# Routing weights for the experts by transposes, DRAM and broadcast loads in place of spreading matmuls

## What is computed

```python
scores = jax.nn.sigmoid(xt.astype(jnp.float32) @ gate_w.T)      # 16 experts
biased = scores + gate_b
_, idx = lax.top_k(biased, TOPK)                                # TOPK = 4
w = jnp.take_along_axis(scores, idx, axis=-1)
w = w / jnp.sum(w, axis=-1, keepdims=True) * ROUTE_SCALE        # 2.5
comb = jnp.zeros((T, N_EXPERTS)).at[jnp.arange(T)[:, None], idx].add(w)
# for every expert e, over all T tokens:
h = _silu_and_mul(xt @ w13_e.T)                                 # 64 inner columns
y = y + c_e[:, None] * (h @ w2_e.T)
# and one shared expert without a weight:
y = y + _silu_and_mul(xt @ w13_s.T) @ w2_s.T
```

## Time and profile before

| | |
|---|---|
| time before, median of 3 runs | 1105.42 us (1102.48 to 1107.36) |
| the profiled execution | 1107.76 us |
| its span, first to last instruction | 1105.8 us |
| mean granted clock of PE | 0.934 |
| busy: PE, PEld, DVE, ACT, POOL | 1010.0, 471.6, 570.1, 558.1, 154.5 us |
| DMA | 27.36 MB in 8542 packets |

### The profile page before, as it was taken

How to read it: one execution, slowest core, us unless ns; L and a number is a source line. 1 busy time by engine, 2 the same in 40 slices (tenths; PEclk the granted TensorE clock), 3 DMA queues, 4 the chain that set the end, 5 groups by cost and what they waited for, 6 DMA issues and landing times.

```text
span 1105.8 us, 21935 instructions
## 1 busy us (share of the span) xinstructions
PE 1010.0 (91%) x9584; PEld 471.6 (43%) x9592; DVE 570.1 (52%) x942; ACT 558.1 (50%) x767; POOL 154.5 (14%) x168
## 2 busy tenths in 40 slices
PE   6679998989999999987989799998999999999998
PEld 3446665343333334775433243433433333353443
DVE  3665663463333447556546454455666665425454
ACT  4213445468999975543645561227454554445111
POOL 2400102023100101111001140000123223104000
PEclk9579999899999999667999899999999999998999
DMA  7654421001000000000000000000000000000000
GB/s 283 191 119 96 100 41 41 1 0 40 2 2 2 2 2 1 3 4 4 0 1 0 1 0 1 0 1 0 2 2 2 2 2 2 1 1 0 10 9 19
DMA packets 8542, 27.36 MB, mean 25 GB/s; under 512 B 3264, under 2 KB 3456, under 8 KB 6784
## 3 DMA queue, kind: packets, MB, share of 16 engines
q1 hardware_dynamic: 8448, 25.97, 8.3%
HBM read 21.44 MB, written 4.29 MB: 23 GB/s over the span
## 4 chain that ended last, share of the span: by engine, by line
PE 78%; DVE 8%; ACT 8%; DMA 3%; issue 2%; SPq 1%; POOL 1%; DVEq 0%; POOLq 0%
PE ps L1516 78%; ACT nrr L734 1%; ACT nrr L732 1%; DMA stf<-aux 1%; DVE mxq L1124 1%; DMA stf<-in_bk 1%; ACT work L979 1%; DVE stf L1484 1%; DMA csb<-in_c 1%; ACT nrr L721 0%; ACT nrr L718 0%; ACT stf L940 0%; POOL work L692 0%; DVE hz L1044 0%; DVE work L1157 0%
## 5 line engine op out<-in xcount | busy, mean ns | idle before, releaser
L1516 PE MATMUL ps<-rq,stf 32*64 32x512 f32 (+4 forms) x4096 | 211.1, 466 | 5.9 <-issue 2.8
L1516 PE MATMUL ps<-work,vbuf 64*32 64x96 f32 (+7 forms) x3200 | 200.0, 406 | 1.9 <-DVE nsq L1207 1.1
L1516 PE MATMUL ps<-hz,wsb 128*128 128x512 f32 (+1 forms) x352 | 160.7, 622 | 4.0 <-ACT nsq L723 3.5
L1516 PEld LDWEIGHTS ps<-rq,stf 32*64 32x64 f32 x4096 | 99.5, 150 | 111.2 <-issue 89.3
L839 ACT ACTIVATE work<-ps 128x1024 f32<-128x1024 f32 x144 | 139.4, 1022 | 13.5 <-PE ps L1516 10.0
L1516 PEld LDWEIGHTS ps<-work,vbuf 128*32 128x32 f32 (+1 forms) x3200 | 72.7, 121 | 114.8 <-issue 63.8
L901 ACT ACTIVATE work<-ps 128x1024 f32<-128x1024 f32 x72 | 73.7, 1025 | 75.6 <-PE ps L1516 75.6
L1516 PE MATMUL ps<-bsb 128*128 128x384 bf16 x256 | 89.8, 352 | 17.7 <-DMA rq<-in_bk 4.7
L778 ACT ACTIVATE work<-ps 128x768 f32<-128x768 f32 x64 | 51.5, 812 | 97.5 <-PE ps L1516 97.1
L1516 PEld LDWEIGHTS ps<-hz,wsb 128*128 128x128 f32 (+1 forms) x352 | 62.8, 190 | 87.3 <-issue 71.6
L948 ACT ACTIVATE work<-ps 128x512 f32<-128x512 f32 x48 | 28.7, 597 | 134.5 <-PE ps L1516 116.3
(11 more groups left out here) (201 smaller groups left out, 1253.2 us busy)
## 6 DMA issues: line engine op xcount, KB each, us to landing
wsb<-in_w SPq DMA_DIRECT2D x1, 3440.0 KB, 16.8
stf<-scr_k SPq DMA_DIRECT2D x12, 204.0 KB
stf<-scr_q SPq DMA_DIRECT2D x12, 192.0 KB
rq<-in_rq SPq DMA_DIRECT2D x2, 1024.0 KB, 5.1
csb<-in_c SPq DMA_DIRECT2D x1, 1619.0 KB, 9.8
scr_q<-work SPq DMA_DIRECT2D x6, 256.0 KB, 3.5
scr_k<-work SPq DMA_DIRECT2D x6, 256.0 KB, 4.8
rq<-scr_k SPq DMA_DIRECT2D x6, 204.0 KB
```

The costliest lines, as they stand in the source:

```text
L1516: return nc.tensor.matmul(o, l, r, start=start, stop=stop, skip_group_check=True)
```

## The change

The routing weights no longer pass through bf16 parts and a spreading matmul. PE transposes `cw` in fp32, four transposes for each chunk, in `route_rows(c)` between the last steps of `ahead`. ACT copies the 16 rows to SBUF (`cwt`, in `rows(c)`). SP stores the chunk's rows to DRAM (`scr_w`, 16 by 2048), waits for the store, and loads them for each pair into one of SHARES = 8 buffers of 128 partitions by 512 tokens: row 2j on partitions 0 to 63, row 2j + 1 on 64 to 127. From the ninth load on, a load waits until DVE has used its buffer. DVE multiplies by that buffer instead of a PSUM bank. The parts, their steps on DVE, the memsets on POOL, the bf16 transposes, the spreading matmuls and their constant go away.

```diff
-        comb = stf[:, 0:T // 2].bitcast(BF16)
+        cwt = stf[0:NE, 0:T]
+        share = stf[:, 2 * T:2 * T + SHARES * CH].rearrange("p (k s) -> p k s", k=SHARES)
...
+        scr_w = nc.dram_tensor("scr_w", (NE, T), F32, kind="Internal").ap()
...
-        ROUTE_STEPS = 16
+        ROUTE_STEPS = 12
+        ROUTED = 5
...
+            def shares(i):
+
+                def store(c):
+                    sp.wait_ge(m_cs, NC * i + c + 1)
+                    sp.dma_start(scr_w[:, c * CH:(c + 1) * CH], cwt[:, c * CH:(c + 1) * CH]).then_inc(m_st[c], 16)
+
+                def load(c, j):
+                    k = (i * NC + c) * NPAIR + j
+                    if k >= SHARES:
+                        sp.wait_ge(m_h, k - SHARES + 1)
+                    sp.dma_start(share[:, k % SHARES], scr_w[2 * j:2 * j + 2, c * CH:(c + 1) * CH].unsqueeze(1)
+                                 .broadcast_to([2, HB, CH])).then_inc(m_w[k % SHARES], 16)
+
+                store(0)
+                sp.wait_ge(m_st[0], 16 * (i + 1))
+                for j in range(NPAIR):
+                    load(0, j)
+                for c in range(1, NC):
+                    store(c)
+                for c in range(1, NC):
+                    sp.wait_ge(m_st[c], 16 * (i + 1))
+                    for j in range(NPAIR):
+                        load(c, j)
...
             rope_load(1)
+            shares(0)
+            shares(1)
...
             def moe_layer(i):
-
-                pool.wait_ge(s_res, 4 * (U_LOC, U_AR)[i] + 4)
-                nc.gpsimd.memset(cparts, 0.0).then_inc(m_z, 1)
-                pool.wait_ge(m_z, 2 * i + 1)
-                nc.gpsimd.memset(comb[96:P, :], 0.0).then_inc(m_z, 1)
-                pool.wait_ge(m_z, 2 * i + 2)
...
+                def rows(c):
+                    act.wait_ge(m_t, NC * i + c + 1)
+                    nc.scalar.activation(cwt[:, c * CH:(c + 1) * CH], bank(4 + c)[0:NE], ACT.Copy).then_inc(m_cs, 1)
...
-                for c in range(NC):
-                    act.wait_ge(m_t, NC * i + c + 1)
-                    nc.scalar.activation(comb[0:96, c * CH:(c + 1) * CH], bank(4 + c)[0:96], ACT.Copy)\
-                        .then_inc(m_cs, 1)
+                    if ROUTED < a <= ROUTED + NC:
+                        rows(a - ROUTED - 1)
...
-                rest = s_
-                after()
-                done(nc.vector.tensor_copy(cparts[:, :, 0, 0:NE], cw))
-                after()
-                done(nc.vector.tensor_tensor(rest, cw, cparts[:, :, 0, 0:NE], ALU.subtract))
-                after()
-                done(nc.vector.tensor_copy(cparts[:, :, 1, 0:NE], rest))
-                after()
-                done(nc.vector.tensor_tensor(cparts[:, :, 2, 0:NE], rest, cparts[:, :, 1, 0:NE], ALU.subtract))
...
-                            dve.wait_ge(m_gu, k + 1)
-                            nc.vector.tensor_tensor(moe[:, 2, k % 2], bank(spread_bank(c, j)), hidden_of(2 + j),
+                            dve.wait_ge(m_w[k % SHARES], 16 * (k // SHARES + 1))
+                            nc.vector.tensor_tensor(moe[:, 2, k % 2], hidden_of(2 + j), share[:, k % SHARES],
                                                     ALU.mult).then_inc(m_h, 1)
...
                         dve.wait_ge(m_su, full(i, c, j) + 1)
-                        nc.vector.tensor_tensor(moe[:, 2, k % 2], bank(spread_bank(c, j)), moe[:, 1, k % 2],
+                        dve.wait_ge(m_w[k % SHARES], 16 * (k // SHARES + 1))
+                        nc.vector.tensor_tensor(moe[:, 2, k % 2], moe[:, 1, k % 2], share[:, k % SHARES],
                                                 ALU.mult).then_inc(m_h, 1)
...
-                    mm(bank(2 + k % 2), w_("w_up")[:, j * P:(j + 1) * P], ch(z, c))
-
-                def spread(c, j):
-
-                    k = (i * NC + c) * NPAIR + j
-                    if k - 1 > i * NC * NPAIR:
-                        pe.wait_ge(m_h, k - 1)
-                    mm(bank(spread_bank(c, j)), b_("spread")[:, j * P:(j + 1) * P], ch(comb, c)).then_inc(m_gu, 1)
+                    mm(bank(2 + k % 2), w_("w_up")[:, j * P:(j + 1) * P], ch(z, c)).then_inc(m_gu, 1)
+
+                def route_rows(c):
+                    pe.wait_ge(m_d, ROUTE_STEPS * (i + 1))
+                    for tt in range(4):
+                        ins = nc.tensor.transpose(bank(4 + c)[0:NE, tt * P:(tt + 1) * P],
+                                                  rt[:, (4 * c + tt) * NE:(4 * c + tt + 1) * NE], c_("ident"))
+                    ins.then_inc(m_t, 1)
...
                 for a in range(AHEAD):
                     ahead(a)
-                pe.wait_ge(m_d, ROUTE_STEPS * (i + 1))
-                for c in range(NC):
-                    for tt in range(4):
-                        ins = mm(bank(4 + c)[0:96, tt * P:(tt + 1) * P],
-                                 cparts[:, 4 * c + tt].rearrange("p i e -> p (i e)"), b_("ident"))
-                    ins.then_inc(m_t, 1)
-                pe.wait_ge(m_cs, NC * (i + 1))
-                spread(0, 0)
+                    if ROUTED <= a < ROUTED + NC:
+                        route_rows(a - ROUTED)
...
                             gate_up(*todo[n_ + 1])
-                        spread(*todo[n_ + 1])
                     if j == 0:
+                        pe.wait_ge(m_cs, NC * i + c + 1)
                         shared_down(c)
```

More of the change, by code:

```diff
@@ L56 @@
 NORMS = 13
+SHARES = 8
 LANE = 20
@@ L83 @@
          ("near", P * (2 * KT - 1))]
-BCOLS = [("ident", 128), ("band_q", 2 * W_A), ("band_a", 2 * W_A),
-         ("spread", NPAIR * 128)]
+BCOLS = [("ident", 128), ("band_q", 2 * W_A), ("band_a", 2 * W_A)]
 def columns(spec):
@@ L164, in build @@
         dacc = stf[:, 2 * T:3 * T]
-        comb = stf[:, 0:T // 2].bitcast(BF16)
+        cwt = stf[0:NE, 0:T]
+        share = stf[:, 2 * T:2 * T + SHARES * CH].rearrange("p (k s) -> p k s", k=SHARES)
         moe = work[:, 0:12 * CH].rearrange("p (k m s) -> p k m s", k=6, m=2)
         rt = stf[:, T:T + 2048]
-        cparts = stf[:, 2 * T:2 * T + 768].bitcast(BF16).rearrange("p (t i e) -> p t i e", i=3, e=32)
         early = aux[:].rearrange("p (j s) -> p j s", j=6)
@@ L269, in build @@
         m_t = sem("route_transposed")
-        m_z = sem("route_room_zeroed")
-        m_cs = sem("route_stack")
+        m_st = [sem(f"route_stored{c}") for c in range(NC)]
+        m_w = [sem(f"share_loaded{n}") for n in range(SHARES)]
+        m_cs = sem("route_rows")
         s_ws = sem("shared_down_weights_copied")
@@ L412, in outputs @@
             return 4 * (u - (u > U_LOC)) + c + 1
-        def spread_bank(c, j):
-            return 4 + (c + 1 + (c + j) % 2) % 4
         def full(i, c, j):
@@ L944, in moe_layer @@
                         k = (i * NC + c) * NPAIR + j
-                        act.wait_ge(m_gu, k + 1)
+                        act.wait_ge(m_gu, full(i, c, j) + 1)
                         if full(i, c, j) >= 2:
@@ L1378, in moe_layer @@
                 after()
-                dve.wait_ge(m_z, 2 * (i + 1))
                 done(nc.vector.scalar_tensor_tensor(out=cw, in0=w8, scalar=ROUTE,
@@ L2105, in bfloat_constants @@
     put("band_a", np.tile(np.where(ok, 0.0, NEG), (1, 2)))
-    spread = np.zeros((P, NPAIR, 2, INTER), np.float32)
-    for e in range(NE):
-        for part in range(3):
-            spread[32 * part + e, e // 2, e % 2, :] = 1.0
-    put("spread", spread.reshape(P, -1))
     return c.astype(BF16_NP)
```

## The result

| | before | after |
|---|---|---|
| median | 1104.2 us (4 runs, 1102.48 to 1107.36) | 1276.35 us (4 runs, 1269.34 to 1277.72) |
| profiled execution | 1107.76 us | 1277.72 us |
| its span | 1105.8 us | 1275.6 us |
| mean granted clock of PE | 0.934 | 0.881 |

The kernel after takes 1.157 times as long, with a 95% interval of 1.153 to 1.160. The forecast was 1291 us and its range 1250 to 1350.

What follows compares the result with a forecast made beforehand. PE, busy 91% of the span, was taken as the bound; waits for 5.48 us loads add 2 x (91.3 + 1.5) = 185.6 us to the profiled 1107.8, giving 1293, as median 1291; range 1250 to 1350.

Steps and rivals of the forecast that it cites:

- Two engines for a load: Expert-layer weight loads: outermost source dimension 2 puts all 32 loads of a layer on the same 2 DMA engines.
- The price of a packet: Weight loads: 0.0854 us for each 2 KB packet, taken from the last store of x.
- 5.48 us a load: Each weight load on 2 engines: 64 x 0.0854 + 0.015 = 5.48 us, forecast range 4.9 to 6.4.
- a sum near 1230: Whole kernel, estimated from the specified 27 GiB/s an engine and 4.5 us a load; not used for the forecast.
- The first product: Layer start: rows copied 657.5, stored 659.3, first packet 660.1, then a 5.48 us load and 0.4 completion.
- The bubble between loads 8 and 9: Load 9 waits for three stores behind the first eight loads: 0.4 + 0.8 + 0.1, 1.3 us more.
- The low clock: Last down matmul and start of what follows at PE's lowered clock: 1.5 us a layer, bounds 0 and 3.
- The sum: Both expert layers: last product 91.3 us later plus 1.5 for the clock, 2 x (91.3 + 1.5) = 185.6 us.
- The rivals: Weight loads: sixteen engines (1085 us, chance 0.07), four engines (1113, 0.04), or a slower pair (1388 to 1484, 0.09).
- Sixteen engines: Rival for the weight loads: 0.7 us a load, PE stays the bound, 1085 us; chance 0.07.
- The 10 us a layer: Sixteen-engine rival's gain: 5.2 us from full steps, the rest from chunk 1 starting near 669.6 instead of 674.2.
- The sign turns: Weight loads: the change goes from gain to loss at a load of some 2.6 us.

Runs made afterwards that it cites:

- e2: Kernel after with the rows stored twice, so a load's outermost dimension is 4 (4 engines): 1113.19 us, 1.009 of the kernel before.
- e1: Kernel after with each load split into two DMAs of 64 partitions, outermost dimension 64 instead of 2: 1092.72 us, 0.991 of the kernel before.
- e5: Kernel after with the two experts of a pair on alternate partitions, one DMA a load, outermost dimension 64: 1091.31 us, 0.990 of the kernel before.
- e7: Kernel after with the rows stored four times, so a load's outermost dimension is 8 (8 engines): 1098.24 us, 0.997 of the kernel before.
- e4: Kernel after with loads of 128 different rows of x, outermost dimension still 2, routing weights left out: 1274.93 us, 1.156 of the kernel before.
- e10: Kernel after with all 128 partitions loaded from one row, 16 engines, second expert's weight left out: 1092.63 us, 0.991 of the kernel before.

## Why the prediction was right, step by step

**Two engines for a load: shown.** The completion packets (two a load), the share of 0.13 and the doubling in e2 say so, and e1 and e5 undo the whole loss by the outermost dimension alone. Counted in the same way, against the 3264 small packets of before and with 16 for each store, a load has 4 completion packets in e2, 8 in e7 and 16 in e5. The Trainium skill's rule ("DMA: Bandwidth & Descriptors", section "Why a DMA increments its semaphore by 16 and not by 1") gives 2, 4, 8 and 16 engines for after, e2, e7 and e5, and the traces agree at each.

**The price of a packet: the step that was mis-sized.** "5.48 us a load" measured 5.22 us. That term was the packets' busy time, taken as if it were elapsed time. But packets on one engine overlap a little: for 710 to 800 the queue's share of 13.1% of 16 engines is 2.10 busy engines where only two work, so the busy time is 1.05 times the elapsed. 5.48 / 1.05 = 5.23. The earlier trace rows had the clue, a share of 1.06 in 9 to 12 us. The 64 loads come out 64 x 0.26 = 16.7 us shorter, and 1291 - 16.7 = 1274, 2 us from the median. An engine moves 128 KB in 5.22 us, 25.1 GB/s. The same page of the Trainium skill has, under "Specifications", some 27 GiB/s for an engine, from which the prediction estimated 4.5 us for a load and a sum near 1230; the measurement decides for the slower one.

**The first product: right, with terms that cancel.** Forecast 666.0, measured 665.41. These rows of the kernel after show the parts (ACT, then SP, whose second number is the time of all issues of the row together):

```profile
654.78 0.60 ACT L958 ACTIVATE work<-ps 128x512 f32<-128x512 f32 x1 [1.07 <-PE ps L1526]
...
655.75 0.57 ACT L951 ACTIVATE stf<-ps 16x512 f32<-16x512 f32 x1
```

```profile
656.35 0.33 SPq L553 DMA_DIRECT2D scr_w<-stf  x1
657.94 29.74 SPq L559 DMA_DIRECT2D stf<-scr_w  x8
687.72 6.09 SPq L553 DMA_DIRECT2D scr_w<-stf  x3
```

The rows are copied at 656.32, not 657.5: the layer starts 0.86 earlier in this execution, which is within the scatter of such starts and says nothing of the smaller constants, and four transposes cost PE 0.44 (the Silus of ahead stand 2.16 apart, 654.78 and 656.94, instead of 1.72) and not 0.6. Store to load issue is 1.59 (forecast 1.8). But issue to product is 7.47 where 0.8 + 5.48 + 0.4 = 6.7 was put: with the load at 5.22 the two latencies are 2.2 us together and not 1.2. The excess is at the start of the load. The DMA view of 657.9 to 661.9, in slices of 0.1 us, has the first two packets in the slice that begins at 659.3, 1.4 us behind the issue, and the next 0.5 later:

```profile
GB/s 0 0 0 0 0 0 0 0 0 0 0 0 0 0 41 0 0 0 0 41 41 41 82 41 41 41 82 41 41 41 82 41 41 41 82 41 41 41 82 41
```

The 0.8 had been read off a store; the store of the rows shows it again (issued at 656.35, first packet at 657.18), the loads don't.

**The bubble between loads 8 and 9: right in kind, 1.87 us and not 1.3.** The stores of chunks 1 to 3 are issued from 687.72 and come out behind the eight loads; the ninth load is issued at 702.03, right behind the eighth product at 701.95, and its product is at 709.04, 7.09 later. The 0.6 more is the same latency again: the ninth load's first packets start at 703.32, 1.3 behind its issue.

**The low clock: 1.5 us a layer forecast, 0.95 seen** from the last product to the add (2.86 instead of 1.91) in either layer; in the first, half of it is made up for before the second routing step. PE's waits hold its matmuls of the expert stage as well: the clock is 0.84 there, and it costs nothing behind a load of 5.22 us.

**The sum.** Per layer 84.9 (half of 169.8) instead of 92.8: 32 x 0.26 = 8.3 less from the price, and the rest small terms of both signs. One step is 5.90 us (DVE's products at 782.06 and 787.96). In its load the two engines, in step till then, finish 0.7 us apart (786.70 and 787.39), behind an 8 KB packet of the instruction queue (q14) at 785.73; e4 has the same with a step of 5.85. Two other such packets delayed nothing, so that it fell on one of the two engines is likely and not shown.

**The rivals.** Sixteen engines would give 1085, I had said; made so (e1, e5), the kernel takes 1091 to 1093. The 10 us a layer had 5.2 from full steps, which came, and 4.8 from chunk 0, which didn't: the 0.7 us of a load was the price of a store, and the loads of chunk 0 take 1.35 to 1.76. The sign turns where the load passes some 2.6 us, as stated: 2.61 gives 0.9% more (e2), 1.63 gives 0.3% less (e7).

## What to carry to other kernels

Before a broadcast load that SP issues replaces work of an engine, read off its outermost dimension how many DMA engines it gets, and divide: if the load is longer than the step in which it hides, the step becomes the load. An edit that turns `[2, 64, n]` into `[64, 2, n]`, or into two DMAs, can be worth more than the whole change around it: here 1276 became 1091. When a DMA's price is built from busy shares, divide by the share that the same kind of traffic shows at saturation. And take the price of a load from a load: the store of x gave 0.7 us for 256 KB on sixteen engines and 0.8 us from issue to first packet, and the loads here took 1.35 to 1.76 and 1.3 to 1.4.

## What the runs showed of the hardware

- Busy shares of DMA engines pass 1.00: two engines show 2.10 busy over 90 us (13.1% of 16) in the kernel after, so packets on one engine overlap by some 5%.
- Loads of few DRAM rows into 128 partitions stop rising at eight engines: by the mean steps of chunk 0, 50 GB/s at 2 engines, 100 at 4, 160 at 8 and 153 to 178 at 16, while 128 rows of x gave 194. Stores of 256 KB reached 392 on 16. The engines are still counted busy (0.95 to 1.03), so each packet takes longer. What the limit is stays open: rereading does not slow two engines (e4), and it is no rate for each row (e10). Copies further apart in DRAM weren't tried.
- A load of the same shape issued by POOL has 64 packets of 4 KB, 448 of 8 B and 16 of 4 B. A single one moves on two engines (49 GB/s, share 0.13), several at once on different ones (106 GB/s, share 0.39), and one lands in 9.6 us.
- The page counts each reading of a row as a DRAM read: 37.96 MB instead of 21.44, which is 64 loads of 256 KB (16.78 MB) less the 0.26 MB of constants, and the same 37.96 in every experiment. It is a count of what the instructions ask for, so whether anything merges the 64 reads of a row is not shown.
